# Moving nine PSUM copies of attention values from ScalarE to VectorE in the tail of a four-mixer graph network

## What is computed

```python
x = x + L0(h)   # two graph convolutions, then LSTMs over windows of 1, 2, 3 and 4 nodes
x = x + L1(h)   # graph attention (GAT): softmax of leaky(s1 + s2), masked by adj
x = x + L2(h)   # attention: qkv = x @ Wqkv; softmax(q k^T / sqrt(C) + adj, causal) @ v @ Wo
x = x + L3(h)   # spectral mixer: _, U = eigh(L_norm(adj)); U (relu(U^T h W1 + b1) W2 + b2)
```

## Time and profile before

| | |
|---|---|
| median of 3 executions | 978.77 us (974.98 to 979.62) |
| the profiled execution's own time | 979.04 us |
| its span, first to last instruction | 977.3 us |
| TensorE, VectorE, ScalarE, GpSimd busy | 83%, 79%, 51%, 19% of the span |
| mean granted TensorE clock | 0.956 of full speed |

### The profile page before, as it was taken

How to read it: one execution, slowest core, us unless ns; L and a number is a source line. 1 busy time by engine, 2 the same in 40 slices (tenths; PEclk the granted TensorE clock), 3 DMA queues, 4 the chain that set the end, 5 groups by cost and what they waited for, 6 DMA issues and landing times.

```text
span 977.3 us, 13729 instructions
## 1 busy us (share of the span) xinstructions
PE 814.0 (83%) x3856; PEld 541.6 (55%) x3862; DVE 768.1 (79%) x3155; ACT 502.1 (51%) x1106; POOL 182.7 (19%) x444
## 2 busy tenths in 40 slices
PE   4579988888999899999999997579863787696998
PEld 3468874444444466666555554457742565475665
DVE  6867776888888788888887888959989999868433
ACT  0027775554444434434433432268763776695675
POOL 2111111111111111211112121002112331471000
PEclk9999998999999999999999999889995988999799
DMA  8000000000000000000000000000000000000022
GB/s 291 0 1 1 2 1 1 0 1 0 1 1 0 1 1 1 0 1 1 1 1 0 1 1 0 1 1 1 1 1 0 1 1 1 1 1 1 22 72 79
DMA packets 13970, 12.17 MB, mean 12 GB/s; under 512 B 1091, under 2 KB 10822, under 8 KB 13894
## 3 DMA queue, kind: packets, MB, share of 16 engines
q1 hardware_dynamic: 10704, 8.46, 2.6%
q10 hardware_dynamic: 3190, 2.84, 0.9%
HBM read 7.10 MB, written 4.19 MB: 12 GB/s over the span
## 4 chain that ended last, share of the span: by engine, by line
issue 48%; DVE 24%; PE 13%; POOL 12%; ACT 2%; POOLq 0%; DVEq 0%; ACTq 0%
PE bank L642 13%; POOL col_root L414 7%; DVE tt L878 4%; DVE stat L886 3%; DVE HT L878 3%; DVE X L879 2%; DVE uu L878 2%; POOL XI L418 2%; DVE X L878 1%; DVE sm L1002 1%; POOL PP L461 1%; POOL m L461 1%; POOL u L461 1%; DVE sm L1006 1%; POOL t L461 1%
## 5 line engine op out<-in xcount | busy, mean ns | idle before, releaser
L552 ACT ACTIVATE G<-bank,bias 128x512 f32<-128x512 f32 (+1 forms) x252 | 158.4, 636 | 233.4 <-PE bank L642 195.8
L642 PE MATMUL bank<-HT,wih 128*128 128x512 f32 (+1 forms) x504 | 248.5, 579 | 0.3 <-ACT HT L538 0.3
L414 POOL TENSOR_TENSOR col_root<-sa,neg_half 128x1 f32<-128x1 f32 x126 | 79.3, 629 | 486.7 <-DVE sa L880 486.7
L642 PEld LDWEIGHTS bank<-VI 128*128 128x128 f32 x506 | 94.7, 202 | 120.4 <-DVE VI L878 57.9
L642 PE MATMUL bank<-H,whh 128*128 128x512 f32 (+1 forms) x288 | 135.0, 550 | 2.8 <-DVE H L878 2.8
L642 PE MATMUL bank<-VI 128*128 128x129 f32 (+63 forms) x506 | 95.8, 273 | 22.6 <-DVE VI L878 22.5
L512 ACT COPY T<-bank 128x512 f32<-128x512 f32 x128 | 74.8, 585 | 66.7 <-PE bank L642 48.1
L508 ACT ACTIVATE T<-X,nbias,rstd 128x128 f32<-128x128 f32 x256 | 104.7, 486 | 5.1 <-DVE nbias L879 5.1
L642 PEld LDWEIGHTS bank<-XI,A 128*128 128x128 f32 x252 | 40.9, 201 | 89.7 <-DVE A L879 88.3
L652 PE MATMUL bank<-ident,T 128*128 128x128 f32 x256 | 41.5, 292 | 58.3 <-ACT T L583 49.7
L642 PEld LDWEIGHTS bank<-HT,wih 128*128 128x128 f32 x504 | 79.9, 193 | 9.9 <-issue 3.9
(11 more groups left out here) (338 smaller groups left out, 1588.6 us busy)
## 6 DMA issues: line engine op xcount, KB each, us to landing
out_x<-T SPq DMA_DIRECT2D x16, 256.0 KB, 2.3
wih<-in_WihT ACTq DMA_DIRECT2D x1, 1024.0 KB
whh<-in_WhhT ACTq DMA_DIRECT2D x1, 1024.0 KB
qkvT<-in_WqkvT ACTq DMA_DIRECT2D x1, 192.0 KB
wg<-in_Wg ACTq DMA_DIRECT2D x2, 64.0 KB
l3w<-in_L3W ACTq DMA_DIRECT2D x2, 64.0 KB
adj<-in_adj SPq DMA_DIRECT2D x1, 64.0 KB, 2.1
adjT<-in_adjT ACTq DMA_DIRECT2D x1, 64.0 KB
```

The lines of the kernel that those rows point to most:

```text
L414: e.tensor_tensor(out=col["root"][:, :], in0=sa[:, 0:1], in1=neg_half[:, :], op=ALU.pow).then_inc(root_ready, 1)
L552: e.activation(G[x.h][:, gate, 0:n], gate_bank(k)[:, 0:n], ACT.Tanh if gate == 2 else ACT.Sigmoid, bias=bias[:, 4 * (x.p - 1) + gate:4 * ( ...
L642: mm = lambda out, l, r, start=True, stop=True: e.matmul(out, l, r, start=start, stop=stop)
```

## The change

A constant `VALUES_BY_VECTOR` is worked out: the first attention group whose scores are at half 50 or later, that is behind the second eigenvalue pass (two halves more than `block_ends()[-1]`, which is 48). The scores of g7 are half 51, those of g6 half 49, so it is 7. For the nine groups g7 to g15 the copy of the values (128 x 512, f32, PSUM to SBUF) is taken out of ScalarE's slot and put into VectorE's queue, right behind the scores of the same group, with the same wait (`q_v`: TensorE has written the values) and the same signal (`q_vs`). Groups g0 to g6 stay as they were.

```diff
+VALUES_BY_VECTOR = next(k for k in range(NG) if HALF.index(("scores", NG + k)) >= block_ends()[-1] + 2)
@@ ScalarE, in the slots
-                if this and not this.gat:
+                if this and not this.gat and this.g < VALUES_BY_VECTOR:
                     e.wait_ge(q_v, this.g + 1)
                     copy(values[this.g % 4], bank[3 * (this.g % 2)], q_vs)
@@ VectorE, in the halves
                 if kind == "scores" and not x.gat:
                     att_scores(x.g)
+                    if x.g >= VALUES_BY_VECTOR:
+                        e.wait_ge(q_v, x.g + 1)
+                        e.tensor_copy(out=values[x.g % 4][:, :], in_=bank[3 * (x.g % 2)][:, :]).then_inc(q_vs, 1)
```

## The result

The changed kernel took 980.17 us (median of 20), the kernel before 978.05 us (median of 20). The ratio is 1.0027, with a 95% interval of 1.0018 to 1.0035: 1.8 to 3.4 us slower, 2.6 us in the middle. The forecast was 2.2 us more (981.0 us against the 978.77 shown), within a range of 977.0 to 985.0.

A forecast was written before the change was run, and what follows sets the result against it. The prediction took GpSimd to bound until the last pivots, VectorE until Z, TensorE behind. Profiled 979.04 + 1.83 (serial chain) + 0.3 (cover) + 0.1 (behind Z) - 0 gave 981.3, or 981.0 us from the 978.77 median; range 977.0 to 985.0.

The forecast's parts named there:

- What bounds the kernel now: Last 135 us: VectorE's eigenvalue arithmetic, GpSimd until the last pivots, VectorE until Z, then TensorE; ScalarE has room.
- The copy's cost: Each 128 x 512 PSUM copy on VectorE takes 0.69 us and holds its queue 0.61 us start to start.
- 1.83 us in the serial chain: Between last pivots and Z: copies of g13, g14, g15 in VectorE's in-order queue add 3 x 0.61 us in full.
- ScalarE's relief worth nothing: ScalarE loses nine copies, 4.4 us of its queue, from g7 on; claimed gain at the end: 0.
- The cover before the last pivots: VectorE's pauses of 1.65 us from g11's scores, less two copies, leave 0.43; lateness costs 0 to 0.55, taken 0.3.
- the upper case of my sum: Half clock behind TensorE's wait for g7's copy: next turn 1.6 us late, g11's scores 1.0 late, 0.55 on the path.
- rival C: TensorE's half clock lasts longer after longer pauses and slots lose cover: over 0.5% slower; chance of 983 to 987 us 0.12.
- Behind Z: From Z to the end: TensorE's longer pause may prolong its half clock, put in at 0.1 us.
- The signs: Profile after: copy rows near 0.69 us, GpSimd's blocks unchanged, pivot wait 0.3 us or less, Z 1.8 to 2.4 later.
- A: Between last pivots and Z: copies fall into VectorE's small gaps or run at SBUF rate; 978.8 to 979.9 us, chance 0.12.
- B: Six copies between 850.8 and 882 hold up GpSimd's recurrence, 4.1 us on top of 2.2, so 985; chance 0.06.
- D: Slots run ahead because ScalarE is relieved: up to 4.4 us less, 974.4 us; chance 0.02.

The follow-up runs named there:

- the doubled copies: The changed kernel with VectorE's copies of g13, g14 and g15 made twice, the first into scratch; ratio 1.0055 against the kernel before.
- the late copies alone: The kernel before with only the copies of g13, g14 and g15 moved to VectorE, g7 to g12 staying on ScalarE; ratio 1.0026.

## Why the prediction was right, and where a term was off

- **"What bounds the kernel now"** held: VectorE from the last pivots to Z, TensorE behind it. Its 7.06 us of waiting for Z were in my own rows, but I used them only for the clock and not as work that could be placed.
- **The copy's cost**, 0.69 us and 0.61 start to start, came out at 0.68, with a slope of 0.59 from the doubled copies. The SBUF rate, the lower bound of 0.35 us, is ruled out for PSUM; the Trainium skill, "VectorE: DVE Perf Modes", section "Why PSUM operands drop a tier", has f32 out of PSUM at the plain rate, and the 0.68 us agree.
- **1.83 us in the serial chain**: 1.69 in both pairs of profiles, 1.8 with the late copies alone. The missing 0.1 is no copy: in profiles in which VectorE doesn't wait for the last pivots, the chain to Z is that much shorter with no late copy in it (18.89 against 19.02), and against 18.89 the three cost 1.82. Right place, right size.
- **ScalarE's relief worth nothing**: no stretch gets shorter by more than 0.1 us in the profiles with ScalarE's copies gone. ScalarE now waits longer instead (for TensorE, 9.95 us before the turned weights of g14, against 7.80 of waiting before).
- **The cover before the last pivots** was the step that was mis-sized. I gave it 0 to 0.55 us and took 0.3; it was 1.38 and 1.35 in the two profiles. The lateness of TensorE behind g7 (5.4 us foretold, 5.45 measured) and its half clock in the two pieces behind were in the upper case of my sum, in which the scores of g11 come 1.0 us late and 0.55 us reach the path. The runs with full clock in the slot of g9 have these numbers: scores of g11 0.9 to 1.0 us later than before, pivots at 36.5 to 36.6, 0.5 us later. But this agreement is in part luck: the run with only the late copies moved had its scores of g11 0.8 us late as well, with TensorE at half clock for longer and no moved copy ahead of it, so the moved copies themselves account for some 0.2 us there. The rest, 0.9 us, goes with a second half-clock stretch in the slot of g9: the scores of g11 were 1.70 us late in the changed kernel. I had that only as part of rival C ("the half clock lasts longer, and the slots run out of cover"). It was seen only with the copy of g7 on VectorE, and there in four of seven profiles. What decides between the executions stays open.
- **Behind Z**: 0.1 us foretold; 0.10 and 0.24 measured in the two pairs.
- **The signs** that I had named: the copy's row, GpSimd's recurrence to within 0.5 us in all, the vanished wait and the closing stage came as stated. Z was to come 1.8 to 2.4 us later and came 3.07 later behind the recurrence's start, all of the excess from the cover.
- **The sum by profiles** is 3.2 us (1.38 + 1.69 + 0.10), the median difference 2.1, the middle of the interval 2.6. Where the half clock falls moves single executions by up to 2 us behind Z: with the turn of Z in its old place, that turn to the last sum took 68.6 to 68.7 us where the mean granted clock of the first twelve us was 0.74 to 0.77, and 70.2 to 70.75 us where it was 0.52 to 0.57. So one pair of profiles can't be the mean. The median agrees with 2.2 better than the profile does; with a cover term that was a us short in both profiles, that closeness is luck.
- **The rivals**: A (gaps swallow the copies) fell with the "to Z" times. B (GpSimd held up) fell for PSUM sources; with SBUF sources there is such an effect, at some 0.1 us a copy, a third of what that run's expectation gave. C was right in kind, not large enough to reach 0.5%. D (ScalarE's relief) didn't show.

## What to carry to other kernels

Before work moves from an engine with room to another, look at what the receiver's queue is at that very place: a copy cost its full 0.6 us three times because it stood in the serial chain, and didn't lengthen that chain when it stood behind its end. A copy that signals a buffer free must not be queued behind a long block of unrelated work, since the engine that waits for the buffer comes late: here TensorE, by 5.4 us. In the profiles its half-clock stretches lasted longer then, though they did so in some executions without that wait too. And where the trace shows an engine waiting 7 us for one result, look first at what stands behind that wait and could run in it, and leave something for the next wait (here TensorE's for the copies of U): one output moved ahead of it gave 4.9 us, twice what the change had taken, and both outputs only 2.1.

## What the runs showed of the hardware that I hadn't expected

- A 128 x 512 f32 copy from SBUF to SBUF on VectorE (two took 0.75 us together) lengthens GpSimd's small instructions beside it from 0.20 to 0.27 us; with twelve of them the recurrence took 37.20 us, 1.2 us more than with twelve copies of the same size out of PSUM (35.99), for which no such effect was seen. The Trainium skill, "Advanced Engine Details and Errata", section "VectorE Performance Modes", says that two-port VectorE instructions and GpSimd block each other: the trace agrees in kind, if these copies, at 0.37 us each against 0.68 out of PSUM, are such; the price was some 0.1 us a copy.
- TensorE's granted clock turned the time of the slots into a matter of chance, worth 1 to 2 us: the same output product took 1.05 to 1.16 us in some executions and 1.90 to 2.08 in others, and the mean granted clock of the ten us behind the recurrence's start was 0.83 in two profiles and 0.66 in the twelve others.
